# Attention by single key tiles for two heads at once, with the low score product in half of TensorE's rows

## The reference

```python
xn = ln(x, g_norm)
q  = l2norm((xn @ Wq) in 16 heads of 64) * q_scale
k, v = split(xn @ Wkv);  k = l2norm([null_k, k]) * k_scale;  v = [null_v, v]   # one key/value head for all
sim = q @ k.T * 8 + bias(head, i - j)          # bias: a small MLP of the distance i - j
sim = where(key in the future, -max, sim)      # causal; the null key is always seen
out = softmax(sim) @ v
z   = ln(out @ Wout, g_out)
y   = x + ternary_linear(int8-style rounding of z)
```

## Time and profile before

| | |
|---|---|
| median of three runs | 1911.69 us |
| span of the profiled execution, first to last instruction | 1909.3 us |
| TensorE busy (matmuls) | 1637.2 us, 86% |
| VectorE busy | 1605.8 us, 84% |
| GpSimd busy | 1329.1 us, 70% |
| ScalarE busy | 1167.9 us, 61% |
| mean granted TensorE clock | 0.969 |

### The profile page before, as it was taken

The page is one execution under the profiler, slowest core; times in us unless marked ns, Lnnn a source line. Parts: engine busy times, 40 slices in busy tenths (PEclk is TensorE's granted clock), DMA queues, the critical chain, the costliest instruction groups (busy, mean ns, idle before and its releaser), DMA issues.

```text
span 1909.3 us, 46551 instructions
## 1 busy us (share of the span) xinstructions
PE 1637.2 (86%) x15098; PEld 1088.9 (57%) x15122; DVE 1605.8 (84%) x2569; ACT 1167.9 (61%) x2195; POOL 1329.1 (70%) x806
## 2 busy tenths in 40 slices
PE   3786996988988988988995887889889889889897
PEld 2343553666666666665552554666666666666553
DVE  5885996999999999996664898799999999999576
ACT  1433654777777777777441555677777777777542
POOL 3554675877777777777672676677777778778575
PEclk9997997999999999999997999899999999999998
DMA  5001110001001001000022001000100100100022
GB/s 174 1 0 26 28 56 20 25 24 47 23 26 44 23 31 39 23 23 11 28 71 91 28 27 58 25 25 23 47 23 23 47 23 23 47 23 0 12 72 94
DMA packets 28411, 69.49 MB, mean 36 GB/s; under 512 B 8368, under 2 KB 8880, under 8 KB 24240
## 3 DMA queue, kind: packets, MB, share of 16 engines
q1 hardware_dynamic: 23712, 60.22, 9.9%
q10 hardware_dynamic: 4640, 8.54, 1.3%
HBM read 60.21 MB, written 8.54 MB: 36 GB/s over the span
## 4 chain that ended last, share of the span: by engine, by line
PE 33%; issue 28%; DVE 19%; POOL 16%; DVEq 1%; POOLq 1%; ACT 0%; DMA 0%; ACTq 0%; SPq 0%
PE ps L1103 18%; PE ps L1125 14%; DVE work L900 10%; DVE work L910 6%; POOL rinv L458 3%; POOL work L463 3%; POOL work L490 3%; POOL qo L421 2%; POOL work L508 2%; PE ps L1161 1%; DVE work L926 1%; POOL rstd L453 1%; POOL work L466 1%; POOL work L429 1%; PE ps L1082 0%
## 5 line engine op out<-in xcount | busy, mean ns | idle before, releaser
L479 POOL TENSOR_TENSOR work<-work 128x1024 f16<-128x1024 f32 x448 | 885.9, 1997 | 267.2 <-ACT work L611 261.6
L611 ACT ACTIVATE work<-work 128x1024 f32<-128x1024 f32 (+1 forms) x640 | 608.9, 966 | 296.5 <-DVE work L900 296.4
L900 DVE SCALAR_TENSOR_TENSOR work<-ps,tab 128x1024 f32<-128x1024 f32 (+1 forms) x640 | 697.3, 1110 | 80.1 <-PE ps L1103 77.1
L1103 PE MATMUL ps<-qo,kT 128*128 (+1 forms) x2560 | 607.5, 360 | 115.9 <-DVE work L900 109.3
L1125 PEld LDWEIGHTS ps<-vals,work 128*128 128x128 bf16 (+1 forms) x8704 | 546.3, 98 | 128.8 <-ACT work L611 11.5
L1125 PE MATMUL ps<-vals,work 128*128 128x129 f16 x8704 | 601.5, 220 | 1.9 <-POOL work L479 1.9
L1103 PEld LDWEIGHTS ps<-qo,kT 128*128 128x128 f16 x2560 | 216.4, 98 | 273.2 <-DVE work L900 77.0
L910 DVE TENSOR_TENSOR work<-work 128x1024 f16<-128x1024 f32 x192 | 292.1, 1521 | 0.0
L1071 PE MATMUL ps<-wq,work 128*128 128x512 f16 x768 | 178.0, 390 | 20.5 <-DVE work L829 20.5
L1161 PE MATMUL ps<-wout,work 128*128 128x512 f16 x768 | 172.9, 382 | 0.0
L618 ACT ACTIVATE work<-null_v,p_null 128x65 f32<-128x65 f32 x512 | 135.2, 335 | 9.9 <-DVE work L931 9.9
(11 more groups left out here) (129 smaller groups left out, 1570.6 us busy)
## 6 DMA issues: line engine op xcount, KB each, us to landing
tab<-bias_table SPq DMA_DIRECT2D x32, 1088.0 KB, 5.6
work<-in_x SPq DMA_DIRECT2D x64, 256.0 KB, 2.7
out_x<-work ACTq DMA_DIRECT2D x32, 256.0 KB, 2.8
work<-in_L_cond_Wq SPq DMA_DIRECT2D x1, 2048.0 KB, 12.5
work<-in_L_cond_Wout SPq DMA_DIRECT2D x2, 1024.0 KB, 10.3
qo<-in_L_cond_w SPq DMA_DIRECT2D x1, 1024.0 KB, 8.7
qo<-in_L_cond_b SPq DMA_DIRECT2D x2, 256.0 KB, 4.2
qo<-in_L_cond_g SPq DMA_DIRECT2D x2, 256.0 KB, 4.5
```

Source lines behind the costliest of these rows:

```text
L479: pool.tensor_tensor(low[:, k % LRING, :, c0:512], probs[:, r, :, c0:512], high[:, r, :, c0:512], ALU.subtract).then_inc(low_pool, 1)
L611: act.activation(probs[:, k % RING, :, c0:512], probs[:, k % RING, :, c0:512], ACT.Exp).then_inc(expd, 1)
L900: dve.scalar_tensor_tensor(out=dst, in0=ps[:, 2 * (k % 2):2 * (k % 2) + 2, c0:512], scalar=SCORE, in1=t_ap, op0=ALU.mult, op1=ALU.add).the ...
L1103: last = pe.matmul(ps[:, 2 * (k % 2) + e, c0:512], kT[:, a, j * P:(j + 1) * P], qT[:, bass.ds(h, 1), 512 * i + c0:512 * i + 512].squeeze(1 ...
```

## The change

The loop over heads becomes a loop over pairs of heads (`HP` = 8), and a unit is one key tile j of block i for both heads of the pair. Each unit still fills two PSUM banks, now one per head. There are 40 units for two heads, as there were 40 pairs. The blocks run from the last to the first. On the diagonal, the unit's first 128 (j - 4i) queries are left out, so that the last four units of a block have 512, 384, 256 and 128 columns.

The product of k's low half with q's low half is left out: the second product of a head takes 64 rows, k_low with q_high. So that both heads' second products lie in different rows of the array, stage B writes q as (high, low) for even heads and (low, high) for odd ones (`q_part`), and the matmul is given the row position 0 or 64.

The eight sums of a block (two heads by four tiles) stand three to a bank in three banks, and these move round the four banks 4 to 7 (`sum_bank`). They are drained bank by bank, the first one unit earlier than the other two. The pairs whose low half VectorE makes go from 6 of 20 to 4 of 40. `tab` holds the current two heads' table, loaded in four slices of 512 columns (512 KB each), each as soon as its block is through. TensorE's loop over heads becomes straight code within a batch. The waits inside are adapted to the new counts.

```diff
-TW = S + P
+TW = S
+NEARER = (0, 1, 5, 9)
-PAIRS = [(i, q) for i in range(NB) for q in range(2 * i + 2)]
-NP = len(PAIRS)
+HP = H // 2
+BLOCKS = tuple(reversed(range(NB)))
+UNITS = [(i, j) for i in BLOCKS for j in range(4 * i + 4)]
+NU = len(UNITS)
...
-DVE_LOW = (2, 5, 8, 11, 14, 17)
-LASTS = {PAIRS.index((i, 2 * i + 1)): i for i in range(NB)}
+DVE_LOW = (4, 10, 22, 32)
+SUMS = 3
+SUM_TILES = (range(0, 3), range(3, 6), range(6, 8))
+LASTS = {UNITS.index((i, 4 * i + 3)): i for i in BLOCKS}
+NULLS = {UNITS.index((i, 4 * i + 1)): i for i in BLOCKS}
+DONE = {UNITS.index((i, 4 * i + 2)): (i, (0,)) for i in BLOCKS} | {
+    UNITS.index((i, 4 * i + 3)): (i, (1, 2)) for i in BLOCKS}
+def unit(k):
+    i, j = UNITS[k]
+    return i, j, P * max(0, j - 4 * i)
+def turn(i):
+    return NB - 1 - i
+def sum_bank(i, q):
+    return 4 + (SUMS * turn(i) + q) % 4
...
+                with sp.Fori(0, HP) as hp:
+                    for k, i in LASTS.items():
+                        sp.wait_ge(biased, (b * HP + hp - 1) * NU + k + 1 + CB)
+                        sp.wait_ge(tab_ld, 16 * ((b * HP + hp) * NB + turn(i)) + 16)
+                        src = bass.AP(table.tensor, hp * (2 * TABW) + 1 + P + 512 * i, [[1, P], [TABW, 2], [1, 512]])
+                        sp.dma_start(tab[:, :, 512 * i:512 * i + 512], src).then_inc(tab_ld, 16)
...
+                def bias(hp, k):
+                    i, j, c0 = unit(k)
+                    if i == BLOCKS[0] and j in NEARER:
+                        dve.wait_ge(tab_ld, 16 * ((b * HP + hp) * NB + NEARER.index(j) + 1) + 16)
                     dve.wait_ge(scored, n + 1)
                     dve.wait_ge(pv_done, n + 1)
...
+                def drain(hp, k):
+                    i, done = DONE[k]
+                    m = (b * HP + hp) * NB + turn(i)
+                    dve.wait_ge(pv_done, (b * HP + hp) * NU + k + 1 + RING)
+                    for q in done:
+                        t0, n = SUM_TILES[q].start, len(SUM_TILES[q])
+                        acc = ps[:, sum_bank(i, q), 0:n * VS].rearrange("p (t d) -> p t d", d=VS)
+                        dve.tensor_tensor(denom[:, i % 2, t0:t0 + n], acc[:, :, 2 * DH],
+                                          null_tmp[:, i % 2, t0:t0 + n, DH], ALU.add).then_inc(o_den, 1)
+                        dve.tensor_tensor(o_part[:, t0:t0 + n, :], acc[:, :, DH:2 * DH],
+                                          null_tmp[:, i % 2, t0:t0 + n, 0:DH], ALU.add).then_inc(o_low, 1)
+                        if q == 2:
+                            dve.wait_ge(o_den, 3 * m + 3)
+                            dve.reciprocal(rec[:, i % 2, :], denom[:, i % 2, :]).then_inc(o_rec, 1)
+                        dve.wait_ge(o_low, 3 * m + q + 1)
+                        dve.tensor_tensor(o_sum[:, i % 2, t0:t0 + n, :], acc[:, :, 0:DH], o_part[:, t0:t0 + n, :],
+                                          ALU.add).then_inc(o_added, 1)
+                def heads(hp, first):
+                    for k in range(NU):
+                        bias(hp, k)
+                        if k - 2 in DVE_LOW:
+                            low_part(hp, k - 2)
+                        if k >= LAG + 1 and k - LAG - 1 in DONE:
+                            drain(hp, k - LAG - 1)
...
                     pe.wait_ge(biased, n - 1 + CB)
                     for e in range(2):
-                        for a in range(2):
-                            j = 2 * q + 1 - e
-                            last = pe.matmul(ps[:, 2 * (k % 2) + e, c0:512], kT[:, a, j * P:(j + 1) * P],
-                                             qT[:, bass.ds(h, 1), 512 * i + c0:512 * i + 512].squeeze(1),
-                                             start=a == 0, stop=a == 1)
+                        pe.matmul(ps[:, 2 * (k % 2) + e, c0:512], kT[:, 0, j * P:(j + 1) * P],
+                                  qT[:, 2 * hp + e, 512 * i + c0:512 * i + 512], start=True, stop=False)
+                    for e in range(2):
+                        last = pe.matmul(ps[:, 2 * (k % 2) + e, c0:512], kT[e * DH:(e + 1) * DH, 1, j * P:(j + 1) * P],
+                                         qT[e * DH:(e + 1) * DH, 2 * hp + e, 512 * i + c0:512 * i + 512],
+                                         start=False, stop=True, tile_position=(e * DH, 0))
                     last.then_inc(scored, 1)
...
+                        for t in range(8):
+                            e, s, q = t // 4, t % 4, t // SUMS
+                            if s < j - 4 * i:
+                                continue
+                            if part == 0 and j == 0 and t % SUMS == 0:
+                                pe.wait_ge(o_added, 3 * m + q + 3)
+                            last = pe.matmul(
+                                ps[:, sum_bank(i, q), (t % SUMS) * VS:(t % SUMS + 1) * VS],
+                                parts[:, rings[part], e, s * P:(s + 1) * P], vals[:, j, :],
+                                start=(part == 0 and j == 0 and t % SUMS == 0),
+                                stop=(part == 1 and j == 4 * i + s), skip_group_check=True)
                     last.then_inc(pv_done, 1)
...
+                for hp in range(HP):
+                    for k in range(NU):
+                        score(hp, k)
+                        if k >= LAG:
+                            weigh(hp, k - LAG)
+                        elif hp:
+                            weigh(hp - 1, k - LAG + NU)
```

## The result

The changed kernel takes 2012.72 us against 1911.34 for the one before, each the median of four runs on one chip: a ratio of 1.053, interval 1.052 to 1.055. Forecast were 1838 us and a range of 1765 to 1935. The change is slower by 101 us, and the forecast had the wrong sign.

The account below looks back on a forecast made before the run. It took TensorE and VectorE, near full and waiting for each other, as the bound; 53.3 + 10.5 + 3.0 = 66.8 us a round against 71.2, 16 rounds plus 3.4 us at stage ends, gave 1838 us, range 1765 to 1935.

Parts of the forecast that it names:

- TensorE's work: Score matmuls 22.0 us plus sums 31.3 us per two heads: 53.3 us, against 62.4 before.
- waits at four block changes: TensorE's stalls for bank drains at the head of each block: 10.5 us a round, ends 6 to 11.
- waits behind VectorE's low parts: TensorE stalls when a VectorE low-part subtraction is blocked: 3.0 us a round, in place of the present 8.8.
- Form switches: TensorE changing between 128-row and 64-row matmuls, 80 times a round: taken as 0, at most 0.26 us each.
- rival C: The array empties at each change of form: slower, 1982 us at 0.16 us a switch, 2071 at 0.26; chance 0.15.
- The new wait: In a block's first unit, second and third groups of sums wait for VectorE's drains: 2.7 us per block change.
- Three streams: The two 64-row products run beside each other, so a unit's scores cost three streams: 22.0 us a round, not 29.4.
- rival B: The 64-row halves run in turn, not side by side: 72.0 us a round, 1921 us; chance 0.15.
- Low parts: VectorE's four low-part subtractions a round, means near 2.3 us: three stall TensorE 0.9 us each, the fourth 0.3.
- GpSimd: GpSimd's work per two heads rises from 55.4 to 60.6 us, yet stays below the round's period.
- Rival A: Block changes cost little, stalls overlap and GpSimd bounds: 62 us a round, 1762 us; chance 0.17.
- The end of a stage: Sums left behind the last score fall from 71 to 44: about 1.7 us less, twice, 3.4.

Follow-up runs that it names:

- the drains first: The changed kernel with VectorE draining the sum banks ahead of the bias add of the same step, not behind it: 1850.17 us.
- the first wait filled: The changed kernel with 11 repeats of the opening matmul ahead of only the first wait at each block change: 1935.91 us.
- the run with both waits filled: The changed kernel with 11 and 26 repeats of the bank-opening matmul ahead of the two waits at each block change: 1935.27 us.
- the last version: Second product in 128 rows, third bank drained later and its sums made last; VectorE makes two low parts a round in place of four: 1806.89 us.
- the run with 128 rows: The changed kernel with the second score product of both heads in 128 rows, so four streams and no change of form: 2001.58 us.

## Why the prediction was wrong

Forecast 66.8 us a round, measured 78.45: 11.65 too little. Step by step, per round:

| step | forecast | measured | off by |
|---|---|---|---|
| TensorE's work, changes of form in it | 53.3 | 62.5 | +9.2 |
| waits at four block changes | 10.5 | 8.7 | -1.8 |
| waits behind VectorE's low parts | 3.0 | 0.56 | -2.4 |
| half clock behind the block changes | no term | 6.0 | +6.0 |
| rest | | | +0.7 |

The 62.5 is TensorE's busy time in a round of 67.4 us at full clock, with the drains first. The 6.0 is the changed kernel's round less that with the first wait filled (78.45 - 72.4); the rest is what the other rows leave. Of the 9.2, changes of form are 8.1; most of the other 1.1 is an effect of the records, in which the last matmul before a wait counts as busy for about 0.16 us (an estimate from the earlier trace rows) beyond its pace. Counted from start to start, the two waits of a block change come to 2.5 us, and those of a round to 10.0.

- *Form switches, "I take 0": the first step that failed.* A switch costs 0.10 us: 0.205 in a full unit (0.85 for 0.645), 5.7 us over the 28, and 2.4 in the twelve trimmed ones, 8.1 a round. A full unit takes 1.78 us, not the 1.56 that the forecast named as its sign. The argument, that alternating kinds of matmul at full pace shows no cost, was about matmuls of one form, so it wasn't the nearest row. The range had it (0 to 0.26), and rival C named the place. The runs show the price, and not whether the array's emptying or the exposed load makes it. C decided from 0.08 us by its own sum; it held, though its 0.16 and more did not.
- *The half clock: a term that was missing, and the second step that failed.* The forecast counted two gaps at each block change and never asked what they do to the clock: 6.0 us a round. This was the larger surprise: 77 us of the 101, by the run with both waits filled. Without it the change would still lose 1.3%, through the switches and the waits.
- *The new wait* was right in place, cause and nearly in size: 2.2 us idle, or 2.5 from start to start, where 2.7 were worked out; the drain of a bank took 0.72 us, 0.7 forecast. It was also the key: order on VectorE alone, the same work, gave 162 us back.
- *Three streams* was right, and rival B wrong: the halves run beside each other, 0.21 us saved per full unit. The Trainium skill, "TensorE: Matmul & The Clock Gate", section on packing small matmuls, has matmuls in different row groups run concurrently; the trace agrees (0.32 us against 0.53). The Trainium skill, "TensorEngine Tiling (Array Packing)", key properties, says that changing the tiling mode drains the engine; the 0.10 us at each change agrees with it, but a load no longer hidden would give as much.
- *Low parts.* Fewer of them on VectorE is probably where the change gained: with ten of 40 in place of four, drains first, the round is 11.7 us longer. 3.0 us overstated what is left: only one of four made TensorE wait. Their mean was 1601 ns, not 2.3 us: of a round's four two ran alone (1.22 us), one met GpSimd in part (1.55) and one in full (2.54). The longer round isn't the reason, since with the drains first it is 67.3 us and the mean 1579.
- *GpSimd* was busy 59.4 us a round, 60.6 foreseen. *Rival A* had the wrong time, but its bound is near what the last version reaches: 64.2 us, with GpSimd at 38 of 40 low parts and busy 61.4. Which engine bounds that version was not tested.
- *The sum over rounds.* Eight rounds of 7.25 us would lose 58 us a batch; 50 were lost. From first score to first score the first round of a stage takes 68.5 us in the changed kernel, 69.3 before: it gains 0.8, and seven rounds of 7.25 less that are 50. With the first wait filled the first round takes 68.4 and 69.3 us in the two batches, so nothing comes back there. Seven rounds of 6.0 are 42 us a batch, and the profiled executions differ by 84 us in all (2010.9 and 1927.3); the times of that kernel vary from 1929.7 to 1940.2 us, and its median is 77 below the change. The end of a stage is shorter, as foreseen.

What brings the clock down stays open. Two waits of 0.68 and 1.53 us with three matmuls between them did, and a single one of 3.52; single ones of 1.80 and 1.5 did not. In the run with 128 rows waits of 0.78 and 1.53 us did once and did not another time, so the length and number of the gaps alone don't decide it. The finer trim was measured with the drains first (26 us); the walk over two heads, the four bank rotation and the block order were not taken apart from each other.

## What to carry to other kernels

Reusing an accumulator bank sooner makes its drain part of the consumer's critical path: put the drain ahead of whatever the same engine does that waits for work queued behind it, but not so early that the engine waits for the sums. Count a gap on TensorE once for its length and, where the clock falls behind it, a second time, and look at the granted clock of each stretch before other explanations. Two changes of form cost as much as one stream of 512 columns; by these prices (an estimate, no run groups them) halves of the array pay only where several matmuls of that form follow each other.

## What the runs showed of the hardware

- Adding matmuls made the kernel faster: 148 more per round, 77 us less; with them the clock stayed at 1.00 (2.4 GHz) behind the block changes.
- A change between 128-row and 64-row matmuls costs 0.10 us each way, with 512 columns and with 128: first products of 128 columns took 0.21 us to the next start (603.10 to 603.31 below), where two streams of 128 would be 0.11 by the pace of the earlier trace rows (an estimate).
- A pair of 64-row matmuls in different rows takes one stream, in the same rows two (0.32 and 0.53 us for 512 columns, with the change back).
- The weight load of the next form starts 0.01 us ahead of its matmul at a change of form, 0.22 us ahead without one.

```profile
603.10 0.27 PE L1131 MATMUL ps<-qo,kT 128*128 128x128 f16 x2
603.31 0.23 PE L1135 MATMUL ps<-qo,kT 64*128 64x128 f16 x2
603.47 1.08 PE L1158 MATMUL ps<-vals,work 128*128 128x129 f16 x16
```
